# A graph layer on one core: a smaller scratch for GpSimd's transfers, and a longer ring of gathered rows

## The reference

```python
h   = x @ W_in2f                                        # 50000 x 256
Wij = (ssp(rbf @ Wf1 + bf1) @ Wf2 + bf2) * dist_cut     # rbf = edge_attr_64, dist_cut = edge_weight1
x_ij = h[idx_j] * Wij                                   # idx_j = dst, sorted
m   = segment_sum(x_ij, idx_i, 50000)                   # idx_i = src, in no order
m   = ssp(m @ Wo1 + bo1) @ Wo2 + bo2                    # ssp(v) = softplus(v) - log 2
out = layernorm(x + (x + m))
```

## Time and profile before

| what | value |
|---|---|
| time, median of 3 runs | 1828.89 us (1828.09 to 1830.81) |
| the profiled execution | 1837.85 us, its span 1836.1 us |
| mean granted TensorE clock | 0.986 of full speed |
| busy: PE, DVE, ACT, POOL | 1740.3, 1507.6, 1484.6, 1429.4 us |
| moved by transfers | 363.45 MB |

### The profile page before, as it was taken

The page is one execution under the profiler, slowest core; times in us unless marked ns, Lnnn a source line. Parts: engine busy times, 40 slices in busy tenths (PEclk is TensorE's granted clock), DMA queues, the critical chain, the costliest instruction groups (busy, mean ns, idle before and its releaser), DMA issues.

```text
span 1836.1 us, 36487 instructions
## 1 busy us (share of the span) xinstructions
PE 1740.3 (95%) x11376; PEld 1543.6 (84%) x11376; DVE 1507.6 (82%) x3750; ACT 1484.6 (81%) x2945; POOL 1429.4 (78%) x1385
## 2 busy tenths in 40 slices
PE   4989999999999999999999999999978999999995
PEld 3778888888888888888888888888877999999995
DVE  3777877888878888778888788888866999999996
ACT  3777877778787787777787888888757999999996
POOL 5554688888888888888888877777764999999997
PEclk9999999999999999999999999999988999999998
DMA  9999866666666666666666656777655899999994
GB/s 340 373 385 392 218 120 119 114 120 121 115 121 118 119 121 115 122 121 115 121 118 116 119 109 113 155 148 154 127 88 193 288 361 362 360 362 361 362 362 171
DMA packets 177340, 363.45 MB, mean 198 GB/s; under 512 B 25623, under 2 KB 76265, under 8 KB 177149
## 3 DMA queue, kind: packets, MB, share of 16 engines
q1 hardware_dynamic: 101128, 257.75, 40.7%
q0 software_dynamic: 75136, 102.45, 34.0%
q10 hardware_dynamic: 884, 0.92, 0.2%
HBM read 206.90 MB, written 154.12 MB: 197 GB/s over the span
## 4 chain that ended last, share of the span: by engine, by line
PE 23%; POOL 23%; issue 3%; DMA 2%; ACT 1%; DVE 1%; another core or an unknown queue 0%; POOLq 0%; ACTq 0%; DVEq 0%
PE pair L411 15%; POOL sums L387 14%; POOL to_spare L383 5%; PE pair L497 4%; POOL acc L356 2%; PE pair L422 2%; POOL to_spare L381 1%; PE pair L435 1%; PE pair L434 1%; DMA acc<-sums,src_ix 1%; DMA xg<-in_x,dst_t 1%; DVE msg_l L674 0%; ACT zs L584 0%; ACT zs L578 0%; POOL xg L343 0%
## 5 line engine op out<-in xcount | busy, mean ns | idle before, releaser
L356 POOL DMA_INDIRECT acc<-sums,src_ix x392 | 631.9, 1612 | 163.6 <-issue 103.2
L343 POOL DMA_INDIRECT xg<-in_x,dst_t x392 | 394.8, 1007 | 184.8 <-issue 110.3
L387 POOL TENSOR_SCALAR sums<-sums,to_spare 128x256 f32<-128x256 f32 x392 | 283.1, 734 | 10.2
L623 ACT ACTIVATE m_h<-pair,wgt_t 128x256 fp32r<-128x256 f32 x392 | 164.5, 476 | 133.8 <-PE pair L411 98.6
L497 PE MATMUL pair<-m_h,same 128*128 128x256 f32 (+1 forms) x980 | 252.2, 291 | 7.1 <-issue 3.6
L497 PE MATMUL pair<-m_l,same 128*128 128x256 f32 (+1 forms) x980 | 244.8, 284 | 0.0
L411 PE MATMUL pair<-wo_h,msg_h 128*128 128x256 f32 (+1 forms) x784 | 233.5, 298 | 10.7 <-DVE m_l L784 7.3
L497 PEld LDWEIGHTS pair<-m_h,same 128*128 128x128 f32 (+1 forms) x980 | 187.3, 191 | 41.9 <-DVE m_l L784 20.7
L411 PE MATMUL pair<-wo_h,msg_l 128*128 128x256 f32 (+1 forms) x784 | 222.3, 284 | 0.0
L411 PE MATMUL pair<-wo_l,msg_h 128*128 128x256 f32 (+1 forms) x784 | 221.4, 282 | 0.0
L767 DVE SCALAR_TENSOR_TENSOR pair<-pair,bias_w,h_sb 128x512 f32<-128x512 f32 x196 | 147.9, 755 | 89.2 <-PE pair L411 62.2
(11 more groups left out here) (104 smaller groups left out, 5563.2 us busy)
## 6 DMA issues: line engine op xcount, KB each, us to landing
acc<-fill SPq DMA_DIRECT2D x197, 256.0 KB
xg<-in_x SPq DMA_DIRECT2D x97, 512.0 KB
sums<-acc SPq DMA_DIRECT2D x97, 512.0 KB, 6.9
out<-sums SPq DMA_DIRECT2D x97, 512.0 KB, 4.8
attr<-in_edge_attr SPq DMA_DIRECT2D x196, 128.0 KB
srcb<-in_src_rows SPq DMA_DIRECT2D x98, 256.0 KB
xg<-in_x,dst_t POOLq DMA_INDIRECT x392
acc<-sums,src_ix POOLq DMA_INDIRECT x392
```

The costliest lines, as they stand in the source:

```text
L343: pool.indirect_dma_start(xg[0:g.p, g.xs, r], None, t["x"], bass.IndirectOffsetOnAxis(ap=dst_t[0:g.p, r, g.n:g.n + 1], axis=0)).then_inc(x ...
L356: pool.indirect_dma_start(acc, bass.IndirectOffsetOnAxis(ap=src_ix[g.slot][0:g.p, r:r + 1], axis=0), sums[0:g.p, g.slot, r], None, compute ...
L387: last = pool.tensor_scalar(normed[0:g.p, g.n % NRING, r], res[0:g.p, u, r], neg_mean[0:g.p, u, r:r + 1], rstd[0:g.p, u, r:r + 1], ALU.add ...
L623: act.activation(m_h[0:g.p, r], bank[6][0:g.p, k * D:(k + 1) * D], ACT.Copy, scale=col(wgt_t, r, g)).then_inc(mh_sb, 1)
```

## The change

Nothing else is edited; through XRING the loads of `x` for the second stage change as well: the first 19 groups are loaded in the last 19 steps of the first stage. By the formula the gathers of the rounds become 268 in 94 rounds in place of 284: in place of 3 nearly always, 3 in most and 2 in every sixth or seventh.

```diff
-XRING = 16
+XRING = 19
 ARING = 4
 SRING = 2
-AHEAD = 27
+AHEAD = 31
...
-    nc = bacc.Bacc("TRN2", target_bir_lowering=False, num_devices=1)
+    nc = bacc.Bacc("TRN2", target_bir_lowering=False, num_devices=1, dynamic_dma_scratch_size=4096)
```

## The result

The changed kernel takes 1843.88 us (median of 4 runs, 1841.8 to 1845.69), the kernel before 1828.56 us on the same chip: a ratio of 1.0092, 95% interval 1.0074 to 1.011. It is slower by somewhat less than 1%, and lies above the predicted 1830 us and above the range's end of 1838 us.

The account below looks back on a forecast made before the run. The prediction took TensorE's pace to bound the first stage, with PE and ACT busy throughout the second. Its terms, + 3.3 - 2.6 + 0 + 0 = + 0.7 us, gave 1829.6, stated as 1830 us, range 1822 to 1838 us.

Parts of the forecast that it names:

- four more groups: Gathers after the clears: 24.6 us more, first round at 231.8 us, TensorE waiting for none of it, cost nothing.
- The lag: First stage: GpSimd starting 1.8 steps later brings more long TensorE steps; between 1.6 and 4.1 us, taken as + 3.3 us.
- In step from round 77 on, near 1112 us: Sign in the later profile: GpSimd waits for `src_ix` from there, with even steps of 13.19 us only from there.
- The end: Last steps of the first stage: last gathers land sooner, TensorE waits less, - 2.6 us, if GpSimd is in step by round 90.
- 19 places: Three more groups of `x` loaded before the second stage: cost nothing in the steps, give nothing to that stage, 0 us.
- The scratch of 4 KB: Indirect transfers: no row shows a wait for room in the scratch, so 0 us.
- The bound: First stage goes at TensorE's pace, 13.19 us a step; second stage has PE and ACT busy without a gap.
- GpSimd must be in step by the end: Rival, end of first stage: dearer transfers decide once rounds exceed 11.88 us; 1852 us at 0.1 us each; chance 0.13.
- the lag costs more: Rival, first stage: 3.9 us for each step of lag, giving 1833 us, or 1836 with slower gathers; chance 0.17.
- The sum: Whole kernel: + 3.3 - 2.6 + 0 + 0 = + 0.7 us.
- those 9 us: Whole run: runs without a profile have a median 9.0 us below the profiled execution of 1837.85 us.

Follow-up runs that it names:

- e15: The changed kernel again, one execution in a batch of the even kind: 1825.06 us, where the kernel before took 1818.2 us.
- e3: Against the kernel before: 31 groups gathered ahead, 17 ring places, scratch of 12,288 bytes; 1847.95 us against 1836.75, ratio 1.0057.
- e11: The kernel before without the gathers of the rounds, groups 27 to 97 using rows already there; 1811.91 us against 1836.15, ratio 0.9857.
- e9: The changed kernel again, in a batch of the uneven kind: 1846.8 us against 1836.15 for the kernel before, ratio 1.0058.
- e10: 31 groups ahead, 17 places, scratch of 12,288 bytes, against the kernel before in another uneven batch: 1848.65 us against 1836.15, ratio 1.0077.
- e7: Changed kernel with 27 groups ahead and one gather added to each of the first 16 rounds; 1852.12 us against 1821.44 for before, ratio 1.0169.
- e1: The kernel before with only the scratch cut to 4,096 bytes; 1835.89 us against 1836.75, ratio 0.9995.
- e17: Changed kernel, first gather of groups 27 to 30 waiting for the group before to land; 1834.47 us against 1821.09 for before, ratio 1.0075.
- e16: 29 groups ahead, the last two gathered in waiting pairs, 16 more gathers in round 40, 19 places, 4 KB scratch; 1859.51 us against 1835.04 for before.
- e6: Changed kernel with 27 groups ahead and 16 extra gathers in a row in round 40; 1832.39 us against 1821.44 for before, ratio 1.0063.
- e12: The kernel before, unchanged, one execution in a batch of the even kind: 1818.2 us.
- e0: The kernel before, unchanged, run again in a batch of the uneven kind: 1836.75 us.
- e8: The kernel before, unchanged, run again in another batch of the uneven kind: 1836.15 us.
- e2: The kernel before with a scratch of 4,096 bytes and 19 ring places, still 27 groups ahead; 1836.19 us against 1836.75, ratio 1.0001.

## Why the prediction was wrong, point by point

**The step that failed** is that of the four more groups: "TensorE, at step 15, has rows for twice as many groups and waits for none of this." It waits for no rows, but it stops. The gathers that follow one another without a wait hold up TensorE's signals, 17.8 us in steps 13 to 16 where the sum had 0. One assumption hid it: that each group waits for the landing of the one before, 5.90 or 4.88 us after its issue. Those two gathers of the earlier trace rows stand where `x` is being loaded for the second stage, and weren't in light traffic. Behind the clears the last gathers of groups 27 to 29 landed 2.6 to 3.0 us after their issue, by the records of their semaphores (3.4 and 3.5 us for groups 28 and 29 in e15, whose records are complete), and the next group's third gather comes 3.75 us after it at the earliest: so the wait in the program no longer spaced the gathers.

**The lag, + 3.3 us.** Not borne out. With a first round 1.4 steps later (226.63 - 207.15 us), steps 17 to 74 weren't longer, but 12.8 us shorter in the pair of traces. Over the uneven traces with 31 and with 27 groups they were 5.9 us shorter in the mean (782.3 us in four against 788.2 in five); the two sets overlap, and e3 with 31 groups has 789.0. Without gathers the long steps are gone though GpSimd starts as late (e11). Nearly all of them look like the same late signals on a small scale. ScalarE's waits for "remote" before `m_h` in these steps (us, times, longest), in before, from 257 us, and in after, from 275 us, both to 1046 us:

```profile
ACT m_h L623 <- remote: 24.4, 8, 3.3
```

```profile
ACT m_h L623 <- remote: 11.9, 4, 3.3
```

They differ by 12.5 us, the middle by 12.8. The other uneven traces with gathers in the rounds have 15.1 to 23.5 us of them; the nine even traces and e11 have no wait for "remote" at all there. That long steps end where GpSimd comes into step was read rightly from the earlier trace rows; but each long step needs gathers. That the middle gets shorter with fewer of them in the rounds is likely by the means, and not shown.

**In step from round 77 on, near 1112 us.** It looks right and isn't. GpSimd begins to wait in round 77, at 1118.72 us, but for landings and not for `src_ix`; it stays 3.3 to 4.9 us behind its place up to round 92.

**The end, - 2.6 us.** The prediction itself had the condition: "It is given back if GpSimd isn't in step by round 90; by the above it is." In after it wasn't, and the term was given back: the last gathers came late, TensorE waited 2.8 us in step 95, and steps 75 to 96 took 3.8 us more. In the other three uneven traces with 31 groups GpSimd was in step by round 75 (lag 0.0 to 0.3 us), and these steps take 289.7, 290.7 and 290.5 us (e3, e9, e10); the five with 27 groups have 291.4 to 293.6, a mean of 292.8: 2.5 us more. The term has its size where its condition holds.

**19 places, 0 us.** Right for the second stage, which took 450.5 us against 449.0 up to its last store, busy as in the earlier trace rows with a DMA share of 0.98. It had looked only at TensorE's steps for what the loads of `x` cost, which stay at 13.2 us. GpSimd's rounds don't: while it is behind, they stand still beside these loads. That the loads do it is argued from the time at which it begins, and from landings 6 to 8 us after the issue in place of 4; no run leaves them out. Where GpSimd is in step, as in before, the landings beside the same loads take 3.9 to 4.1 us.

**The scratch of 4 KB, 0 us.** Right as a sum and not in its parts. Transfers are issued in 1.625 us against 1.612 (adding) and 1.005 against 1.007 (gathers). But every kernel with 4 KB, e7 apart, stands 2.4 to 2.5 us before its last adding transfer, those with more 0.3; and the program ends 3.4 us after the issue of its last store in place of 7.5. That is - 2.0 us in all, under what e1 could tell (0.9979 to 1.001). What makes either isn't known.

**The bound.** "The first stage goes at TensorE's pace" holds in the uneven kind alone. In the even kind TensorE's steps need 765 us in place of 790 from 17 to 74, and GpSimd's transfers set the end: the rival "GpSimd must be in step by the end" names the right place, though no transfer got dearer. By its own numbers GpSimd's slack at the end was 0.45 us a round; 25 us fewer of TensorE over 58 steps are 0.43 us each, which uses it up. (In the rival "the lag costs more", 2.1 steps of 3.9 us make 1837 us and not 1836; nothing hangs on it.)

**The sum again**, with sizes measured in the pair: stop + 17.8, middle - 12.8, steps 75 to 96 and the end of the stage + 5.4, second stage + 1.5, program end - 4.1, beginning - 0.5: + 7.3 us. The medians of the first result are 15.3 us apart. The other 8.0 us don't lie in the changed kernel: its profiled execution took 1845.12 us, 1.2 above its median, while that of before took 1837.85 us, 9.3 above its median of 1828.56. The prediction took those 9 us for what a profile costs. The other runs don't bear that out, as their profiled executions lie among the rest (e1: 1835.37 us in 1830.51 to 1842.01; e17: 1834.88 us in 1832.82 to 1839.34). So the trace of before is of a slower sort than the times beside it, and no trace shows where those gained. The stop itself varied, from 16 to 38 us over the four traces with 31 groups.

**What stays open.** Why a batch is of the even or uneven kind, with one and the same kernel and, once, one and the same chip. The traces themselves differ too: the uneven ones with gathers in the rounds hold 21,143 to 21,807 records of semaphore changes, the even ones 32,313 to 32,377. So the name "remote" may come from a missing record, and the readings above rest on the waits' lengths and on the steps' times. And what in TensorE's path waits while gathers are issued, the results' writes or the signal.

## What to carry to other kernels

A run of GpSimd's indirect transfers isn't always free for engines that wait for none of their rows: see what all engines do beside the longest unbroken run in the trace, and don't count on a wait for landings to space them, since it vanishes when traffic gets light. Where GpSimd's rounds end in a wait for landings, put the transfers that nobody waits for behind the last one that somebody does: moving three gathers from there cost 14%. Check that an engine that waits once a step is in step: it may wait for its own transfers, still behind. And profile a kernel in several batches before building on its bound: here TensorE was the bound in some and GpSimd in others, with the same program.

## What the runs showed of the hardware

- 19 gathers of 128 rows of 1 KB in a row, one each 1.25 us, held up work between TensorE and ScalarE by 7.91, 9.85 and 4.56 us (e16), at a DMA share of 0.45. The same burst in the even kind (e6) held up nothing.
- The even kind has neither this nor the long steps: 765.4 us for 58 steps (e12) in place of 786 to 790 (before, e0, e8, e1, e2), with the same instructions.
- With TensorE idle from 219.9 to 224.2 us, its clock was granted at half (0.50) in 224 to 229 us, and was back at 1.00 in 240 to 262 us.
- The last adding transfer of a round landed 3.9 us after its issue in round 69 of e15, and 7.4 and 6.4 us after it in rounds 79 and 84, where GpSimd was 17 to 18 us behind and `x` was being loaded.
- The end of the program, from the issue of the last store, took 7.5 us with a scratch of 16 KB, 5.7 with 12 KB and 3.4 with 4 KB. With 16 KB but 284 indirect transfers fewer (e11) it took 3.7 us.
